# Row tiling of two products in a two-layer f32 tower on one Trainium2 core, and a new order of its merged streams

## What is computed

```
q, k, v, u = X @ Wq.T, X @ Wk.T, X @ Wv.T, X @ Wu.T          # 192 -> 192 each
gate = (X @ Wg.T).reshape(B, L, h, 3)                         # 192 -> 36
...
out = normalised heads of q with sums over k v;  h = x + out @ Wo.T
...
h = hidden_states + where(selected by router, attn_out, mix_out)
n2 = _ln(h, g2, b2)
ffn = gelu(n2 @ W1 + bf1) @ W2 + bf2                          # 192 -> 768 -> 192
return h + ffn
```

## Time and profile before

| what | value |
|---|---|
| median of 3 runs | 891.18 us (887.65 to 892.72) |
| the profiled execution | 889.98 us |
| its span, first to last instruction | 888.0 us |
| PE busy | 708.2 us, 80% of the span |
| DVE, ACT, POOL busy | 517.5, 302.0, 244.0 us |
| mean granted clock of TensorE | 0.914 of 2.4 GHz |

### The profile page before, as it was taken

How to read it: one execution, slowest core, us unless ns; L and a number is a source line. 1 busy time by engine, 2 the same in 40 slices (tenths; PEclk the granted TensorE clock), 3 DMA queues, 4 the chain that set the end, 5 groups by cost and what they waited for, 6 DMA issues and landing times.

```text
span 888.0 us, 15483 instructions
## 1 busy us (share of the span) xinstructions
PE 708.2 (80%) x5452; PEld 543.0 (61%) x5453; DVE 517.5 (58%) x1759; ACT 302.0 (34%) x688; POOL 244.0 (27%) x304
## 2 busy tenths in 40 slices
PE   1577477989677998877899875868767989999993
PEld 1436355566457555655756564754456989998892
DVE  6468658873678875657877466891335553333330
ACT  0033232524334263433325343323133423333330
POOL 5222200451013246001434400132001353333332
PEclk9787769999988999987899999897897999999997
DMA  7950000000000000000111100029201232222220
GB/s 244 413 241 1 1 1 0 19 8 1 2 1 28 27 19 8 1 2 1 37 27 13 4 2 1 1 67 351 63 1 29 37 78 42 36 41 38 36 34 9
DMA packets 29893, 43.62 MB, mean 49 GB/s; under 512 B 5355, under 2 KB 24597, under 8 KB 29830
## 3 DMA queue, kind: packets, MB, share of 16 engines
q1 hardware_dynamic: 19250, 30.87, 10.1%
q0 software_dynamic: 8752, 9.07, 6.3%
q10 hardware_dynamic: 1828, 2.84, 0.9%
HBM read 21.36 MB, written 22.09 MB: 49 GB/s over the span
## 4 chain that ended last, share of the span: by engine, by line
PE 59%; DVE 20%; issue 7%; POOL 5%; DMA 4%; ACT 3%; SPq 1%; POOLq 0%; DVEq 0%; ACTq 0%
PE qa L1839 26%; PE qc L1839 24%; PE qc L1842 5%; PE qa L1842 4%; DMA out<-qk_T 3%; DVE mx L1434 2%; POOL arena_w L440 1%; DVE st L1042 1%; DMA mu_row<-in_mu 1%; POOL rs_a L475 1%; DVE arena_b L1387 1%; DVE arena_e L1255 1%; DVE qk_T L1440 1%; ACT big L797 1%; DVE xb L1059 1%
## 5 line engine op out<-in xcount | busy, mean ns | idle before, releaser
L1839 PE MATMUL qc<-arena_w,big 128*128 x468 | 82.8, 327 | 1.4 <-DVE qk_T L1818 1.4
L1839 PEld LDWEIGHTS qc<-arena_w,big 128*128 128x128 f32 x468 | 75.1, 190 | 2.1 <-issue 2.0
L1839 PE MATMUL qa<-arena_b 128*128 128x128 f32 (+2 forms) x688 | 73.7, 289 | 3.0 <-DVE att L1450 2.1
L1839 PEld LDWEIGHTS qa<-arena_b 128*128 128x128 f32 (+2 forms) x688 | 65.0, 192 | 11.9 <-issue 3.0
L1839 PE MATMUL qa<-arena_e,nT 128*128 128x192 f32 (+2 forms) x256 | 71.6, 437 | 0.1
L1008 ACT ACTIVATE big<-qa,arena_b 128x128 f32<-128x128 f32 x156 | 43.0, 374 | 76.0 <-PE qc L1839 68.9
L603 POOL DMA_INDIRECT out<-qk_T x39 | 61.0, 1565 | 21.1 <-POOL spare L602 10.6
L1807 DVE COPY arena_b<-qc 128x256 f32<-128x256 f32 x39 | 16.6, 425 | 84.3 <-PE qc L1842 84.3
L1839 PEld LDWEIGHTS qa<-arena_e,nT 128*128 128x128 f32 x256 | 48.2, 203 | 22.3 <-issue 12.9
L475 POOL TENSOR_TENSOR rs_a<-rs_a,minus_half 128x4 f32<-128x4 f32 x8 | 8.1, 1011 | 179.7 <-DVE rs_a L1055 172.4
L479 POOL TENSOR_TENSOR rs_b<-rs_b,minus_half 128x4 f32<-128x4 f32 x12 | 12.5, 1041 | 149.0 <-DVE rs_b L1055 149.0
(11 more groups left out here) (365 smaller groups left out, 1546.0 us busy)
## 6 DMA issues: line engine op xcount, KB each, us to landing
slots<-xk SPq DMA_DIRECT2D x1, 13192.0 KB, 42.7
arena_e<-in_w SPq DMA_DIRECT2D x8, 579.0 KB, 8.3
arena_w<-in_w SPq DMA_DIRECT2D x8, 576.0 KB, 8.8
qk_T<-slots SPq DMA_DIRECT2D x39, 97.0 KB, 1.9
out<-hb SPq DMA_DIRECT2D x16, 96.0 KB, 1.7
arena_e<-in_w_l SPq DMA_DIRECT2D x1, 804.0 KB
arena_e<-in_W ACTq DMA_DIRECT2D x1, 768.0 KB
out<-qk_T POOLq DMA_INDIRECT x39, 3.5
```

The source lines that it names most:

```text
L1839: return nc.tensor.matmul(o, l, r, start=start, stop=stop)
```

## The change

It contracts the 192 rows of the four projections and of the net's first product as 128 + 64. Chunk 0 is rows 0 to 127, chunk 1 rows 64 to 191, stored overlapping in both operands. Two outputs are made together: output 0 takes all of chunk 0 and then the upper 64 rows of chunk 1, output 1 all of chunk 1 and then the lower 64 of chunk 0. The two 64-row products follow one another and lie in different halves of the array. For the projections the two outputs are the 384 and the 420 columns of a block, for the net two runs of 128 hidden values; `ffn_up` does both in its even call. The lists of all four engines are rearranged. The order within each of the two streams stays, and so do the lists of `back`. The transposed inputs go to new places (`x1T` in `arena_b`, `n4T` in `qk_T`), and the scale and bias of the net's norm get the overlapping layout too.

```
-                for k, (lo, hi) in enumerate(((0, 384), (384, 804))):
-                    i = both(PS[b % 2][:, k, 0:hi - lo], lambda c: nT[:, c, tok(b)], lambda c: w_l0[:, c, lo:hi])
+                spans = ((0, 384), (384, 804))
+                for k, (lo, hi) in enumerate(spans):
+                    mm(PS[b % 2][:, k, 0:hi - lo], x1T[:, k, tok(b)], w_l0[:, k, lo:hi], True, False)
+                for k, (lo, hi) in enumerate(spans):
+                    r = (slice(KX, 2 * KX), slice(0, KX))[k]
+                    i = mm(PS[b % 2][:, k, 0:hi - lo], x1T[r, 1 - k, tok(b)], w_l0[r, 1 - k, lo:hi], False, True)
                 inc(i, "proj")
...
             def ffn_up(tb, j):
+                if j % 2:
+                    return
                 w(tb, "n2T", 2)
                 if j >= 4:
-                    w(tb, "gelu", j - 3)
-                inc(both((PD, PC, PD)[j // 2][:, j % 2, :], lambda k: w_up[:, k, j * 128:(j + 1) * 128], lambda k: xT[:, k, :]),
-                    "up")
+                    w(tb, "gelu", j - 2)
+                q = (PD, PC, PD)[j // 2]
+                for k in range(2):
+                    mm(q[:, k, :], w_up[:, k, (j + k) * 128:(j + k + 1) * 128], n4T[:, k, :], True, False)
+                for k in range(2):
+                    r = (slice(KX, 2 * KX), slice(0, KX))[k]
+                    inc(mm(q[:, k, :], w_up[r, 1 - k, (j + k) * 128:(j + k + 1) * 128], n4T[r, 1 - k, :], False, True), "up")
```

The transposes and their evacuations (the others alike):

```
-                        i = tr(part_of(PC, CW, b, c), xb[:, b, c * CW:(c + 1) * CW], 128)
+                        i = tr(part_of(PC, 128, b, c), xb[:, b, KX * c:KX * c + 128], 128)
...
+    def overlapped(m):
+        return np.stack([m[0:KR], m[D - KR:D]], axis=1)
```

More of the change, by code:

```diff
@@ L115, in build @@
         gammar, betar, gatewr, wrr, bf2r = (rows[:, k, :] for k in range(5))
-        cols = sb("cols", [CW, 6, C])
-        g1c, b1c, g2c, b2c, bqc, bkc = (cols[:, k, :] for k in range(6))
+        cols = sb("cols", [KR, 6, C])
+        g1c, b1c, bqc, bkc = (cols[0:CW, k, :] for k in (0, 1, 4, 5))
+        g2c, b2c = (cols[:, k, :] for k in (2, 3))
         bf1c = sb("bf1c", [128, FJ])
@@ L195, in build @@
         assert bt[0] <= 5000
+        x1T = part(arena_b, [0], [C, G * 128])
         ct = [0]
@@ L205, in build @@
         x = sb("x", [128, G, D])
+        n4T = part(qk_T, [0], [C, G * 128])
         xn = sb("xn", [128, G, D])
@@ L329, in chunks, with chunks_128 @@
             return t[0:CW, :, hf * 256:hf * 256 + 256].rearrange("p c (b t) -> p b c t", b=2)
+        def chunks_128(t, hf):
+            return t[:, :, hf * 256:hf * 256 + 256].rearrange("p c (b t) -> p b c t", b=2)
         def half(b):
@@ L670, in x1T_evac @@
                 w(ta, "x1T", 2 * hf + 2)
-                A(chunks(nT, hf), half_of(PB, CW, hf), ACT.Copy).then_inc(*done("xT"))
+                A(chunks_128(x1T, hf), half_of(PB, 128, hf), ACT.Copy).then_inc(*done("xT"))
             def vug_evac(ta, b):
@@ L1628, in joint @@
                 mask(ta, 2, 0)
-                token_dot(ta + 1)
+                token_apply(ta + 1)
+                attend(tb, 0)
                 mask(ta, 2, 1)
-                attend(tb, 0)
                 maxima(tb, 1, 0)
@@ L1653, in joint @@
                 router_dot(ta)
+                attend(tb, 3)
                 router(ta)
-                attend(tb, 3)
                 ln6_stats(tb)
+                ln6_apply(tb)
                 pool_weights(ta)
-                ln6_apply(tb)
                 ranks(ta)
@@ L2517, in biased @@
         return r
[L2519 removed]
+    d["w_l0"] = overlapped(np.concatenate([n["L0_attn_" + k].T for k in ("Wq", "Wk", "Wv", "Wu", "Wg")], axis=1))
     d["w_l0o"] = by_rows(n["L0_attn_Wo"].T)
@@ L2522, in _layout @@
     d["mu"] = n["L0_attn_prior_mu"].reshape(1, D)
-    d["cols"] = np.stack([col(f + k) for k in ("g1", "b1", "g2", "b2", "bq", "bk")], axis=1)
+    pad = ((0, KR - CW), (0, 0))
+    d["cols"] = np.stack([overlapped(n[f + k].reshape(D)) if k in ("g2", "b2") else np.pad(col(f + k), pad)
+                          for k in ("g1", "b1", "g2", "b2", "bq", "bk")], axis=1)
     d["bf1"] = col(f + "bf1", FJ)
```

137 lines of the change are left out of this document (68 added, 69 removed).

## The result

The changed kernel took 910.12 us in the median (four runs, 905.09 to 915.24) against 890.99 of before: 1.0214 times before, 95% interval 1.0186 to 1.0243. It is slower, above the range of the forecast. The profiled execution took 905.09 us with a span of 903.1; the mean granted clock fell from 0.914 to 0.893.

What follows compares the result with a forecast made beforehand. PE was taken to bound the joint passes' projections and net, short dependent steps the later stretches. First pass -2.0, last -0.7, three joint passes -0.2 each, POOL +0.3 each: -2.4 from 889.98 gives 887.6 us, range 884 to 892.

Steps and rivals of the forecast that it cites:

- two half-array products run in the time of one: Projections and net's first product: paired 64-row products run together, giving about 10 us less PE work with switches paid.
- a round trip: Switching PE to half-array products and back, in projections and net: 0.40 us each, between 0.38 and 0.44.
- PE's two waits for ACT: Joint pass: PE waits 1.3 us before the net's second product and 1.2 us more before the scores return.
- the first pass: Projections gain 1.0 us, token statistics lose 0.8, earlier token scalings gain 1.8: -2.0 us.
- what follows the joint passes: Last pass, order unchanged: three net pairs gain 1.4 us, the second evacuation takes back 0.7: -0.7 us.
- The serial halves: Rival: in projections and net the two half-array products run one after the other; 901 us, 4 in 100.
- the free switch: Rival: tiling-mode switches hide behind long streams in projections and net, saving 21 us; 869 us, 4 in 100.
- The forecast's own sign of being wrong: Joint passes differing from 148 to 150.5 us by over 2 us would show the forecast wrong.
- first step: Joint pass up to the first logits: masks ahead of the fifth norm win back lateness, 0.6 us gained.
- Second step: Joint pass after the first logits: 1.0 lost on the norm's chain, 0.5 before the router, other swaps gain 1.1 us.
- ACT's lateness passes on: Rival: late scores and fifth norm cost each joint pass 2.4 us, nothing won back; 894.5 us, 20 in 100.
- PE's gain: Joint pass, projections and net's first product: PE gains 2.5 us, all spent on two waits for ACT.

Runs made afterwards that it cites:

- the ladder: Kernel before with spare matmuls in PE's joint-pass waits, then tiling, the late order and the early order added one by one: 0.9837, 0.9873, 0.9913, 1.0002 times before.
- the early order: New joint-pass lists up to block 2's av1 (PE), block 1's attend (DVE) and o_evac (ACT), POOL throughout, added over tiling and the late order, with spares: 892.0 against 884.1 us.
- with spares: Unread 128x128 matmuls put where PE waits, 53 to 59 per joint pass: kernel before 878.0 us, changed kernel 892.0 us.
- the late order: New joint-pass lists behind block 2's av1 (PE), block 1's attend (DVE) and o_evac (ACT), added over the new tiling, with spares: 884.1 against 881.6 us.
- filled changed kernel: The full change plus 59 unread matmuls per joint pass in its own PE waits, fifth session: 892.0 us, 1.0002 times the kernel before.
- filled kernel before: The kernel before plus 59 unread matmuls per joint pass in its PE waits, fifth session: 878.0 us, 0.9837 times the kernel before.
- the first session's pair: Changed kernel and kernel before, without spare matmuls, as first measured: 910.12 against 890.99 us; joint passes 464.80 against 447.73 us.
- the third session's: Changed kernel and kernel before, unaltered, measured again without spare matmuls: 1.0097 times before; joint passes 465.1 against 456.7 us.
- the tiling of session four: New tiling under the old orders plus 61 unread matmuls per joint pass in PE's waits, against the kernel before: 0.9910 times.
- Two kernels that reach the router within 0.2 us of each other: Changed kernel with old joint-pass order restored behind block 2's av1 on PE (0.9928 times before), or only behind block 3's logits_T (1.0063).

## Why the prediction was wrong

*Right:* that two half-array products run in the time of one, and the 0.4 us of a round trip (2.49 us for a block's projection where I had 2.51, 3.04 for a pair where I had 3.04). So were PE's two waits for ACT (1.16 and 1.05 us, forecast 1.3 and 1.2) with their places to 0.1 us, the first pass (-2.3, forecast -2.0) and what follows the joint passes (-0.5, forecast -0.7). The serial halves and the free switch are out. The forecast's own sign of being wrong came: the joint passes took 153.5 to 156.6 us, over 2 off its 148 to 150.5.

*Wrong, first step:* "After that the order puts the first masks ahead of the fifth norm ... the first logits come near 361.5 against 362.19, 0.6 gained." They came 0.8 us later than before. I had the scores and the scaling of queries 2.0 late and 2.6 of it won back. The scores are 2.1 late and 2.4 us are won back, much as forecast; but the scaling is 3.2 late, for want of a term for the 1.1 us that three coefficient steps lose beside POOL's residual additions. Against the same tiling in the old order the scores are even 4.4 us late, and the ladder shows 2.0 us lost at the first maxima; in all the early order cost 7.9 us in three passes (dips of 1.2 and 1.3 us in two of them included), where I had a gain of some 2.

*Second step:* "The other order swaps give about 1.1." Here lies the larger part: behind the first maxima I had 1.0 and 0.5 lost against 1.1 gained, and 15.8 of the 17.1 us are lost there, 9.2 of 11.9 with spares. In each pass of the ladder the late order lost 2.0 us between the first maxima and the router, and 4.7 in all: the 1.5 was sized well, the 1.1 gained never came (from block to block the maxima of the filled changed kernel's third pass are 10.7 and 9.5 us apart, those of the filled kernel before 10.7 and 9.4).

*Third, missing:* the sum has no term for the clock. I read 1.00 in the windows of the front of a pass and never asked what the 0.92 over the whole pass would do. By the step from 17.1 to 11.9 it is 5.1 us in the first session's pair; in the third session's it has the other sign.

The rival "ACT's lateness passes on" came only in part. Its first sign, a score exponential that ends over 28 us after the first projection, was there (28.9), but the forecast's own numbers had 28.7, so it doesn't tell the two apart; the first logits came at 61.9, just under its 62. It let each pass lose 2.4 us with nothing won back, and 0.8 were lost at that place. PE's gain was real, but only 1.2 of its 2.5 us a pass arrive even in the old order: the second product then waits 0.9 us for the last evacuations, as the third pair hands over both at once.

The same kernel pair gave 1.021 in one session and 1.010 in another. That spares raise the clock and shorten either kernel is shown; why sessions differ in level at all isn't: before took 902.8 us at a clock of 0.909 in one and 891 at 0.914 in the other. The chip differs with the session, and no run sets the two apart.

TensorE: Matmul & The Clock Gate, HAM oscillation — how this bites in real kernels, in the Trainium skill says that waits between bursts of matmuls, there for DMA, let the clock fall, so that each new burst starts slow. The traces here agree, with waits for DVE and ACT: the changed kernel's key products took 5.06 us without spares and 3.60 with them, and the first pass ran at 0.79 without and 0.95 with.

## What to carry to other kernels

A saving on PE in a kernel of short dependent steps is worth what its latest partner lets through: here 1.2 of 2.5 us a pass at the first maxima, and with spares nothing in the time as a whole. An order "made for it" lost over three times that in the joint passes (12.6 us against 3.6). Take new tilings and new orders as two changes, and time each, with the spares and without: here the halves of the order changed places by it. Look at the granted clock of every stretch before pricing one, and before you read a late step as a wait; where the clock dips behind waits, spare matmuls in those waits are cheap to try. They narrowed the spread of some kernels' runs (2.5 us in the changed kernel of session five) and not of others (12 us in the tiling of session four).

## What was not expected of the hardware

Products that nobody reads made the kernel before 1.6% faster; with the tiling, and with spares in the first pass too, it is 2.7%. A dip of the clock cost 1.7 us in one place and 1.3 in another, as much as a pass's whole gain from the tiling. Where it falls differs between kernels and also between executions of one: the first joint pass's projections took 10.97 us in one trace of the kernel before and 12.66 in another. Two kernels that reach the router within 0.2 us of each other had key products of 3.60 and 4.85 us. Small DVE steps on 48 columns went from 0.20 to 0.62 us when they started together with POOL's additions of 192 columns.
